# A macaron transformer layer on eight cores: one pass over the last W_proj block, and layer-norm sums fed by casting DMAs

## The reference

```python
def ffn(x):                          # x is already layer-normed
    h = square(relu(x @ W_fc.T))     # 1024 -> 4096
    y = h @ W_proj.T                 # 4096 -> 1024
    # 5 steps of: mem = 0.9*mem + y - (mem > 1); spike = (mem > 1)
    return sum(spikes) / 5
def attn(x, gamma, Wq, Wkv, Wo):     # causal, one K/V head for 16 query heads
    ...
x = x + 0.5 * ffn(layernorm(x))
x = x + attn(layernorm(x), ...)
x = x + 0.5 * ffn(layernorm(x))
```

## Time and profile before

| | us |
|---|---|
| median of 2 runs | 2271.35 |
| the 2 runs | 2235.97 and 2306.72 |
| the profiled execution, whole program | 2227.68 |
| its span on the slowest core (core 6), first to last instruction | 2226.1 |
| spans of the eight cores | 2203.2 to 2226.1 |
| TensorE busy (matmul) on core 6 | 1461.2 |
| VectorE busy | 790.5 |
| ScalarE busy | 616.8 |

### The profile page before, as it was taken

One profiled execution on the slowest core, in us unless ns is written; L12 is line 12 of the kernel. 1 busy time (PEld: TensorE's weight loads), 2 busy tenths in 40 slices (PEclk: granted clock), 3 DMA queues, 4 the chain that ended last, 5 costly groups with the idle time before them and its releaser, 6 DMA issues.

```text
span 2226.1 us, 20938 instructions; the slowest of 8 cores (2203.2 to 2226.1 us)
## 1 busy us (share of the span) xinstructions
PE 1461.2 (66%) x6149; PEld 574.6 (26%) x6244; DVE 790.5 (36%) x1530; ACT 616.8 (28%) x1644; POOL 82.4 (4%) x159
## 2 busy tenths in 40 slices
PE   0357659999975456344554554455494999999974
PEld 0023224444331112111111111111141444444431
DVE  0331048181635544442222111111245217273634
ACT  0311012020203000246655665666202303030300
POOL 1000100000012000000000000000100000000000
PEclk9979779999997788755555555555596999999998
DMA  9715930303054111045555666666812031413144
GB/s 209 131 48 144 199 92 22 139 20 132 35 197 79 15 29 20 10 76 95 106 106 110 119 117 123 114 115 121 181 74 67 1 132 53 147 48 133 66 165 147
DMA packets 316943, 219.31 MB, mean 99 GB/s; under 512 B 288522, under 2 KB 288650, under 8 KB 302498
## 3 DMA queue, kind: packets, MB, share of 16 engines
q1 hardware_dynamic: 293586, 104.28, 22.2%
q0 software_dynamic: 22096, 105.30, 17.0%
q10 hardware_dynamic: 1152, 8.39, 1.2%
HBM read 142.53 MB, written 25.25 MB: 75 GB/s over the span
## 4 chain that ended last, share of the span: by engine, by line
PE 47%; DMA 17%; DVE 14%; ACT 11%; issue 6%; another core or an unknown queue 3%; DVEq 1%; POOL 0%; SPq 0%; ACTq 0%; POOLq 0%
PE pb L384 14%; PE pb L503 13%; ACT WB L816 9%; DMA WB<-WB 7%; PE pb L710 5%; DMA Q<-wp 4%; DVE acc L332 4%; PE pb L441 3%; PE pb L867 3%; PE pb L593 3%; DMA Q<-wprojT 2%; ACT Q L390 1%; PE pb L788 1%; PE pb L225 1%
## 5 line engine op out<-in xcount | busy, mean ns | idle before, releaser
L384 PE MATMUL pb<-Q,WB 128*128 128x512 bf16 x2006 | 454.7, 384 | 79.8 <-DVE Q L360 51.4
L816 ACT ACTIVATE WB<-pb,ncb 128x512 bf16<-128x512 f32 (+3 forms) x640 | 389.2, 643 | 241.6 <-PE pb L793 127.8
L503 PE MATMUL pb<-HB,Q 128*128 128x512 bf16 x1506 | 340.0, 384 | 44.8 <-DMA Q<-wprojT 31.2
L390 ACT ACTIVATE Q<-pb 128x512 bf16<-128x512 f32 x256 | 152.6, 597 | 752.6 <-PE pb L384 666.0
L788 PE MATMUL pb<-WB,Q 64*128 64x512 bf16 (+3 forms) x320 | 151.0, 493 | 251.8 <-ACT WB L816 246.3
L384 PEld LDWEIGHTS pb<-Q,WB 128*128 128x128 bf16 x2048 | 199.6, 98 | 333.8 <-issue 105.5
L503 PEld LDWEIGHTS pb<-HB,Q 128*128 128x128 bf16 x1536 | 150.2, 99 | 234.6 <-issue 64.2
L393 DVE TENSOR_TENSOR HB<-Q 128x512 bf16<-128x512 bf16 x256 | 105.1, 424 | 192.6 <-ACT Q L390 185.8
L793 PE MATMUL pb<-WB,Q 64*128 64x512 bf16 (+3 forms) x320 | 156.4, 510 | 0.0
L710 PE MATMUL pb<-WB 128*64 128x512 bf16 x544 | 123.1, 628 | 44.1 <-DMA WB<-WB 43.9
L801 DVE TENSOR_TENSOR pb<-pb,tri 128x128 f32<-128x128 f32 x256 | 76.7, 300 | 208.0 <-PE pb L793 192.8
(11 more groups left out here) (94 smaller groups left out, 852.8 us busy)
## 6 DMA issues: line engine op xcount, KB each, us to landing
Q<-wp POOLq DMA_DIRECT2D x72, 1024.0 KB, 5.6
X<-xin SPq DMA_DIRECT2D x8, 1024.0 KB, 38.9
WB<-wfcT POOLq DMA_DIRECT2D x8, 1024.0 KB, 48.3
Q<-wprojT POOLq DMA_DIRECT2D x32, 256.0 KB, 13.2
wp<-Q SPq DMA_DIRECT2D x8, 1024.0 KB, 9.0
wf<-WB ACTq DMA_DIRECT2D x8, 1024.0 KB, 18.0
WB<-wf POOLq DMA_DIRECT2D x8, 1024.0 KB, 20.9
xout<-X SPq DMA_DIRECT2D x32, 256.0 KB, 2.5
```

Of the source, the lines that this page charges most:

```text
L384: P.emit("T", lambda E, par=par, dc=dc, fc=fc: E.matmul(PB[par][:], wfc_t(dc, fc), xn_t(dc)[:], start=(dc == 0), stop=(dc == DC - 1)), inc ...
L390: P.emit("A", lambda E, par=par: E.activation(hh_t(par)[:], PB[par][:], AF.Relu), inc=("a_rl", 1))
L503: st=st, sp=sp: E.matmul(PB[dc][:], wpe_t(par, fcl, dc), h_t(fc), start=st, stop=sp), inc=mark)
L816: b=(bA, bB)[hl], pc=pc, g=g, po=po: E.activation(p2_t(par, pc, hl, N), PB[b][:, 0:N], AF.Exp, bias=ncb[:, pc:pc + 1], scale=1.0, accum_ou ...
```

## The change

It has three parts.

- **The last block is done like the others.** The two-pass form with its marks `t_yh` and its double fetch is gone; the one loop over 8 groups serves all four blocks of both FFNs (fetch in line 427, matmuls in line 447 of the new file). V copies banks 0 and 1 when they are done, and then evaluates the eight spikes of the last block; the first waits for `t_ye`, the end of the last group.
- **The sums before attention** (`ln_stats("a")` only) no longer use V for the cast: G issues a DMA for each of the 32 chunks that reads f32 from `X` and writes bf16 to the same two buffers. It waits for `t_sx` as V did, and for the spike that writes that chunk of `X` (`v_sp`); A's squares get the latter wait too. The rows are added up in banks 0 and 1 instead of 6 and 7, and T waits for the first two spikes of the last block before it begins. V's copies to `stg` stay on V, behind its spikes.
- **G's order:** `wkk` and `wvv` first, then `wq`, then the 32 casting DMAs. All of the weights' DMAs now stand ahead of the sums in G's stream.

```diff
-    def ln_stats(tag, with_t2, xwait=None):
+    def ln_stats(tag, with_t2, xwait=None, sgate=None, banks=(6, 7)):
...
-                P.wait("V", "t_sx", max(0, P.val("t_sx") - 1))
-                P.emit("V", lambda E, dc=dc, tb=tb, par=par: E.tensor_copy(
-                    xb_t(par)[:], xsl(dc, tb * 512)), inc=("v_xb", 1))
+                if sgate is not None:
+                    P.wait("G", "t_sx", max(0, P.val("t_sx") - 1))
+                    P.wait("G", sgate[0], sgate[1](tb, dc))
+                    P.emit("G", lambda E, dc=dc, tb=tb, par=par: E.dma_start(
+                        out=xb_t(par)[:], in_=xsl(dc, tb * 512)),
+                        inc=(f"g_xb{par}", 16))
+                else:
+                    P.wait("V", "t_sx", max(0, P.val("t_sx") - 1))
+                    P.emit("V", lambda E, dc=dc, tb=tb, par=par: E.tensor_copy(
+                        xb_t(par)[:], xsl(dc, tb * 512)), inc=("v_xb", 1))
...
+                if sgate is not None:
+                    P.wait("A", sgate[0], sgate[1](tb, dc))
...
-                P.wait("T", "v_xb")
+                P.wait("T", f"g_xb{par}" if sgate is not None else "v_xb")
...
-        def emit_spike(tb, dc, gate=None):
-            if gate is not None:
-                P.wait("V", gate[0], gate[1])
-            elif dc == 0:
+        def emit_spike(tb, dc):
+            if dc == 0:
                 P.wait("V", "t_ye", tye0 + (tb + 1) * DC)
...
             if tb == NT - 1:
-                tyh0 = P.val("t_yh")
-                for passB in (False, True):
-                    dcs = range(4, 8) if passB else range(0, 4)
-                    for e in range(8):
...
-                ydb = P.val("t_yd") - 3
-                P.wait("V", "t_yh", tyh0 + 9)
...
                 for dc in range(DC):
-                    if dc < 2:
-                        gate = ("t_yh", tyh0 + 9)
-                    elif dc in (2, 3):
-                        gate = ("t_yh", tyh0 + 8 + dc)
-                    elif dc in (4, 5, 6):
-                        gate = ("t_yd", ydb + dc - 3)
-                    else:
-                        gate = ("t_ye", tye0 + (tb + 1) * 8)
-                    emit_spike(tb, dc, gate=gate)
+                    emit_spike(tb, dc)
...
     def attention():
-        ln_stats("a", with_t2=True)
+        vsp_base = P.val("v_sp") - NT * DC
+        vspL = vsp_base + (NT - 1) * DC
...
+        P.wait("T", "v_sp", vspL + 2)
+        ln_stats("a", with_t2=True,
+                 sgate=("v_sp", lambda tb, dc: vsp_base + tb * DC + dc + 1),
+                 banks=(0, 1))
```

More of the change, by code:

```diff
@@ L204, in build_program @@
     P.drain("V")
-    def ln_stats(tag, with_t2, xwait=None):
+    def ln_stats(tag, with_t2, xwait=None, sgate=None, banks=(6, 7)):
+        B0, B1 = banks
         P.wait("V", "g_x", 16 * DC)
@@ new lines, in ffn @@
+            for e in range(8):
+                par = e % 2
+                ge = tb * 8 + e
+                P.wait("G", "t_ye", max(tye0, tye0 + ge - 1))
+                if tag == "f1" and tb == 0 and e >= 2:
+                    P.wait("G", f"s_wp16p{e % 2}", 16 * (e // 2))
+                if tag == "f2" and tb == 0 and e < 2:
+                    P.wait("G", "t_s")
+                if tag == "f1" and tb == 0:
+                    for fl in range(4):
+                        P.emit("G", lambda E, e=e, par=par, fl=fl: E.dma_start(
+                            out=Q3[:, par * 4096 + fl * 1024: par * 4096 + fl * 1024 + 1024],
+                            in_=wprojT[e * 512 + fl * 128: e * 512 + fl * 128 + 128, :]),
+                            inc=(f"g_wp{par}", 16))
+                    P.wait("S", f"g_wp{par}")
+                    P.emit("S", lambda E, e=e, par=par: E.dma_start(
+                        out=wp16[e * 128:(e + 1) * 128, :], in_=wpe_full(par)),
+                        inc=(f"s_wp16p{par}", 16))
+                else:
+                    if tag == "f1" and tb == 1 and e < 2:
+                        P.wait("G", f"s_wp16p{e % 2}", 64)
+                    P.emit("G", lambda E, e=e, par=par: E.dma_start(
+                        out=wpe_full(par), in_=wp16[e * 128:(e + 1) * 128, :]),
+                        inc=(f"g_wp{par}", 16))
+                P.wait("T", f"g_wp{par}")
+                if e == 0:
+                    P.wait("T", "v_h")
+                for dc in range(DC):
+                    if e == 0 and tb > 0:
+                        P.wait("T", "v_sp", vsp0 + (tb - 1) * DC + dc + 1)
+                    for fcl in range(4):
+                        fc = e * 4 + fcl
+                        st = (e == 0 and fcl == 0)
+                        sp = (e == 7 and fcl == 3)
+                        if dc == DC - 1 and fcl == 3:
+                            mark = ("t_ye", 1)
+                        elif e == 7 and fcl == 3 and dc < 2:
+                            mark = ("t_yd", 1)
+                        else:
+                            mark = None
+                        P.emit("T", lambda E, dc=dc, par=par, fcl=fcl, fc=fc,
+                               st=st, sp=sp: E.matmul(
+                            PB[dc][:], wpe_t(par, fcl, dc), h_t(fc),
+                            start=st, stop=sp), inc=mark)
@@ L518, in attention @@
         P.wait("G", "s_wf16", 16 * DC)
-        for dc in range(DC):
-            P.emit("G", lambda E, dc=dc: E.dma_start(
-                out=WB[:, WQP + dc * 1024: WQP + dc * 1024 + 1024],
-                in_=wq[dc * 128:(dc + 1) * 128, :]), inc=("g_wq", 16))
         for dc in range(DC):
@@ L529, in attention @@
                 in_=wvv[dc * 128:(dc + 1) * 128, :]), inc=("g_wk", 16))
+        for dc in range(DC):
+            P.emit("G", lambda E, dc=dc: E.dma_start(
+                out=WB[:, WQP + dc * 1024: WQP + dc * 1024 + 1024],
+                in_=wq[dc * 128:(dc + 1) * 128, :]), inc=("g_wq", 16))
+        P.wait("T", "v_sp", vspL + 2)
+        ln_stats("a", with_t2=True,
+                 sgate=("v_sp", lambda tb, dc: vsp_base + tb * DC + dc + 1),
+                 banks=(0, 1))
         P.wait("V", "g_wq", 16 * DC)
```

122 lines of the change are left out of this document (16 added, 106 removed).

## The result

| | before | changed |
|---|---|---|
| median, us | 2231.47 (30 runs) | 2238.67 (31 runs) |
| lowest, us | 2224.99 | 2230.36 |
| profiled execution, slowest core's span | 2226.1 (core 6) | 2228.2 (core 3) |

The ratio of the changed kernel to the one before is **1.0032, 95% interval 1.0018 to 1.0047**: 7 us slower (4 to 10.5). The forecast was +14.7 us, within 2%, and 2246.5 us. The direction and "within 2%" came out, the size is half of what was forecast. A few executions of either kernel fall into a slower state, one of the two listed ahead of the prediction (2306.72 us) among them; the ratio compares executions outside it.

What follows compares the result with a forecast made beforehand. The prediction saw the last W_proj block bound by weight fetches, then VectorE's spikes. Sums before attention +22.1 us and FFN 2 -7.4 gave +14.7 on a base of 2231.8, so 2246.5 us, range 2222 to 2292.

Steps and rivals of the forecast that it cites:

- The bound before: Last block: W_proj waits for weight fetches, 78.4 us in FFN 1 against 55.4 to 56.4 elsewhere; then VectorE's spikes set the chain.
- where it was free at 695.1: End of FFN 1's four spikes on VectorE before the change, at 695.1 us; forecast 694.4 after it.
- The single pass: Last W_proj block of both FFNs: a group takes about 7.0 us, its 6.2 us fetch hides, 56.4 us in all.
- FFN 1's gain on TensorE buys nearly nothing on VectorE: End of FFN 1: 22 us saved on TensorE buy 0.7 us on VectorE, as eight spikes follow the matmuls.
- The first block of sums hides beside the spikes: Sums before attention: casts first land near 678.5, the first block is done at about 693.9, ahead of VectorE at 694.4.
- That wq comes behind wkk and wvv costs nothing: GpSimd's weight loads before the casts: the new order is free, since wq's scaling stands behind the sums in VectorE's order.
- The other three blocks cannot hide: Sums before attention: 22 chunks in 11 cycles of 4.5 us, 49.5 us; last copy to stg +22.1 us.
- the term L = 3.0 us: Landing time of one casting DMA in the sums: a store's 2.5 us plus 0.5 for cast and software queue.
- Full gain: Rival, both FFN ends: the idle stretches of 22.0 and 28.7 us vanish and spikes cost nothing, -51 us, 2181 us; chance 0.02.
- Slow casts: Rival, GpSimd's queue in the sums: with L = 6 the cycle is 7.6 us, total +57, 2289 us; chance 0.19.
- Quick casts: Rival, sums: cycle 3.7 us or less, or TensorE and copies set the pace; -9 to -17 us, 2219 us; chance 0.11.
- Fetch stalls in the single pass: Rival, last W_proj block: fetches land in 7.37 us, a group takes 8.0 instead of 7.0; +27, 2259 us; chance 0.05.

Runs made afterwards that it cites:

- depth 1 and 2: Casting DMAs in flight: depth 1 is the changed kernel with each cast waiting for the chunk before, 1.0301 to the kernel before; depth 2 is the changed kernel, 1.0032.
- the run with half fetches: Kernel before, but each pass of the last block fetches only the 0.5 MB half it uses, into four buffers; ratio to the kernel before 0.9711.
- half the bytes and the same depth: Kernel before with 0.5 MB half fetches in two buffers, run twice; ratios to the kernel before 0.983 and 0.9894.
- another run: Kernel before's two passes over the last block, with the changed kernel's casting DMAs for the sums; ratio to the kernel before 1.0181.

## Why the prediction was right in direction and wrong in size

- **The bound before.** Right: W_proj of the last block waited for fetches, and behind it VectorE set the end. But the stretches were read on core 6 alone, the slowest core by span. It begins this block 7 us later than the mean (600.7 against 593.5), and in the block itself it was among the quick ones. In FFN 1 its first copy to stg comes 101.1 us after the block's first matmul, where the eight cores have 101.1 to 109.4, mean 105.7; in FFN 2 its 100.4 stand against a mean of 102.2. **This is one step that failed:** the term "where it was free at 695.1" and the start of -7.4 us were the luck of one core with the clock (0.96 in rows 4, against 0.86 on core 0), and they hide 4.6 + 1.8 = 6.4 us of gain. Of the 4.6 some 3 may in turn be the luck of this one execution, as said under the table.
- **The single pass.** Right: it hides its fetches, 55.4 us on every core, and the first spike follows at once. The term took 56.4 and left 55.4 as the low end; the low end came. The row of eight spikes was 36.3 us instead of 37.2. FFN 2: forecast -7.4, measured -11.0, of which 1.8 are the shorter pass and spikes and 1.8 core 6.
- **FFN 1's gain on TensorE buys nearly nothing on VectorE.** Right as a mechanism. The forecast had 22.0 us on TensorE and 0.7 us at the end of VectorE's spikes, and 7.4 us at the first copy to stg, since the casts of the first block fell away there. Measured are 27 us on TensorE and 10.5 at the first copy.
- **The first block of sums hides beside the spikes.** Nearly. The first cast landed 25.2 us after TensorE's end in the mean of the cores (27.4 on core 3) where 21.4 was forecast, so the first copy came at 95.2 instead of 93.7; with the casts ahead of the loads it came at 92.2. **This is a step that failed, a small one:** "That wq comes behind wkk and wvv costs nothing". The 20.6 us for the loads were read in the other order; with the 16 small loads ahead, the large ones start 8.4 us later and the casts queue behind them. It costs up to 3.1 us.
- **The other three blocks cannot hide.** Right, and for depth 1 and 2 the price has the form that was forecast: 97.0 and 49.0 us. **The step that failed here is the term L = 3.0 us,** which added 0.5 us for the cast and the queue to a store's 2.5 us. No run shows such an addition: L measured 2.3. That is below the 2.5 which the prediction gave as the lower end, and a landing under 2.5 was one of its own signs of being wrong. The end itself was core 6's: the same store has medians of 2.2 to 2.5 us on the eight cores of the kernel before. TensorE's pair of matmuls was 1.02, not 0.9, as the granted clock was 0.50 in the whole stretch of the sums (core 3). The cycle was 4.05 instead of 4.5, and the sums 49.0 instead of 52.8: +25.9 where +29.5 was the forecast.
- **The sum.** Of the 9.8 us between +14.7 and the marks' +4.9, the sums' term has 3.6, FFN 2's 3.6, the first copy 3.1; -0.5 lie in the rest. The difference of the medians is 7.2 us, half of the forecast. That the absolute forecast, 2246.5, is off by no more than this is luck in part: its base of 2231.8 was put midway between two numbers, and 2231.47 was measured.
- **The page weighed.** The Trainium skill's fit ("DMA: Bandwidth & Descriptors", "Anatomy of one DMA — SWDGE (gpsimd) path") would give 2.6 us for the 256 KB that a cast reads, an estimate by that page. It came nearer than the prediction's 3.0, and its total of +10 lies at the edge of the interval. Measured is 2.3 us for a cast from SBUF to SBUF, so by the bytes read the fit is high here, while for the 1 MB fetch from memory at 5.39 it was low. By the 128 KB that the cast writes it would give 2.3, also an estimate by that page; which of the two counts no run here separates. The prediction had let the second case decide on the first.
- **The rivals.** Slow casts: excluded by the median landing of 2.3 us. Quick casts at TensorE's pace: excluded by 49.0 us; with four buffers the sums come to 27.7 us, near the 23.1 of VectorE's casts. Full gain: no, and the run with half fetches shows what it would have needed, spikes beside the matmuls. Fetch stalls in the single pass: none.

## What to carry to other kernels

A producer with n buffers delivers a piece every (handover + landing + work) / n, as long as the engines at both ends are quicker than that; work it out from one row of the chain, and compare it with the pace of the engine that it replaces before moving a cheap 0.4 us cast from VectorE to a DMA. A step on the critical path of all cores is read on all cores, and better in more than one execution, since one of them may have been lucky. The time of a queue of loads holds for the order in which it was read. And a gain on one engine is worth what the next engine's row of work leaves of it: the single pass removes the fetch waits and lays four more spikes behind the matmuls, by the marks -19 us; the half fetches remove the same waits and leave the four spikes beside the matmuls, -58 us.

## What the runs showed of the hardware that was not expected

- A casting DMA of 128x512 from f32 to bf16 within SBUF, issued by GpSimd, landed in 2.2 to 2.3 us (medians of a core) with one or two in flight and in 2.4 to 2.6 with four. That is about what the 256 KB store on the hardware queue takes, 2.2 to 2.5 us by core in the kernel before.
- GpSimd issued the 16 small loads of the changed kernel 0.53 us apart, so that the eight large ones behind them began 8.4 us later than before the change.
- The same waits cost different cores differently: in the two-pass block the granted clock was 0.86 on core 0 and 0.98 on core 3, and 16 matmuls behind a wait took 5.31 and 3.63 us. With half the bytes and the same depth the waits were shorter (about 4.6 us of handover and landing), and nearly all matmuls of FFN 1's block were at the full level. Why core 0 fell back in the long waits here, and neither core 3 here nor core 0 in another run did, stays open.
- Eight loads of 512 KB from memory, issued by GpSimd, kept the casts behind them waiting: the first cast landed 14.39 us after its issue on core 3, and 12.1 in the mean of the cores, instead of 2.3.
